# Four slots instead of two for gathered rows and their indices in a fused graph-network kernel

## The chip, the core and the metric

The kernel runs on one core of a Trainium2 chip, in float32 throughout. The core has TensorE (PE), VectorE (DVE), ScalarE (ACT), GpSimd (POOL) and SyncE (SP), which share an SBUF of 128 partitions and a PSUM of eight banks, meet through semaphores, and move data by DMA. The metric is device time in microseconds (us), as the median of several executions. Beside it there is one profiled execution, from which all rows come.

## What is computed

The graph has N = 3125 nodes with F = 64 features and E = 103125 edges, sorted by destination. Four networks follow one another, each with a residual addition and a layer norm:

```python
# 0: message network, edge weight as the edge feature
x = concatenate([h[src], h[dst], e]);  m = relu(x @ W1 + b1) @ W2 + b2
x = layernorm(x + segment_sum(m, dst))
# 1: GIN with edge features (32 per edge)
msg = relu(x[src] + edge_attr @ We + be);  aggr = segment_sum(msg, dst)
h = relu(((1 + eps) * x + aggr) @ W1 + b1) @ W2 + b2    # leaky relu, norm
x = layernorm(x + h)
# 2: three steps x <- A x with A = norm of the edge weights; 3: ten steps
msgs = norm[:, None] * x[row];  x = segment_sum(msgs, col)
agg = segment_sum(h[s] * wn[:, None], d);  h = 0.9 * agg + 0.1 * feat_0
```

Networks 0 and 1 have a function of each edge, so they are computed edge by edge. Networks 2 and 3 only multiply by a fixed sparse matrix, which the kernel builds once as a dense matrix and then multiplies by on TensorE.

## The kernel before

**Stages.** A preparation (to about 105 us) loads the graph, makes tables in DRAM of what a node contributes to an edge (`d_p`, `d_q`; later `d_t1`), and `rec`, four numbers per edge for 808 tiles of 128 edges. Then comes the edge loop of layer 0 (to about 1400 us), a short node phase, the edge loop of layer 1 (about 1438 to 2708 us), a node phase, and the dense products on TensorE (from about 2762 us), which stream a matrix `d_w` of several MB from DRAM.

**An edge loop.** It runs over 101 superblocks of 1024 edges. In numbers, superblock n uses buffer b = n % 2. `edge_loop` writes the first 96 as nested hardware loops: 6 turns of two quarters, each quarter a loop of 4 turns of two superblocks. The last 5 are written out. For each superblock the engines do this, each engine in its own program order and with semaphores between them, two of each kind, one for each b:

- SP: load 8x128 source indices (L441), once the addition of n-2 is done; in layer 0 two loads of `d_q` rows (L447), in layer 1 one of edge attributes (L451); then two copies of 16 edge records from `rec` into `wrec` (L460), once `pair_outer` of n-2 is done.
- POOL: wait for the indices (`idx`) and for TensorE's sums of n-2 (`seg`), then eight indirect DMAs of 128 rows each (L566) into `G[b]`. These are the gathers.
- DVE: `pair_low` (L669 to L671); the addition of PSUM to the gathered rows (L696), which waits for the gather; one-hot matrices of the next superblock (L654, L657); `pair_outer` (L678, L683, L685); then the aggregation (L705), which adds TensorE's sums of 47 columns to `aggT` and waits for `seg` of n.
- ACT: relu in place on the gathered rows (L1028), a copy of the transposed one-hots (L1021) or attributes (L1023), and the eviction of the dense pair (L1037, L1038).
- PE: the transposes of n+1 (L1180, L1185), 32 matmuls that sum the rows by destination (L1212, L1213, after the relu), the products of n+1 (L1195 or L1198), and 16 matmuls of a pair of 16 columns of the dense matrix (L1224).

The dense matrix is made beside the edges: 96 superblocks of layer 0 and 100 of layer 1 each make one pair. After each 8 superblocks ACT stores a finished quarter, 1 MB, to `d_w`.

**What sets the order.** Nothing is scheduled by a planner: each engine's function `superblock` is its order, and the semaphore counts are its ring. DVE first increments the semaphores `agg` and `add` by 1, so that the first two superblocks find free buffers. If the destinations are not as assumed, a fallback path (`general`) runs instead; with this input it does not.

Of the kernel before, what the change touches and what calls it, by code (L numbers as in the profile page):

```python
# [19 lines left out]
N, F, E, ED = 3125, 64, 103125, 32  # L20
P = 128
NB = -(-N // P)
NP = NB * P
SBE = 8 * P
NSB = -(-E // SBE)
# [14 lines left out]
SPAN = 47  # L40
PIECE = 4
# [18 lines left out]
NC_HT, NC_DEG, NC_LEAKY, NC_X2 = 11, 19, 24, 41  # L60
# [11 lines left out]
def build(nc, x, src, dst, eattr, ew, ew1, W1_0, b1_0, W2_0, b2_0, We, be, W1_1, b1_1, W2_1, b2_1,  # L72
# [5 lines left out]
    with ctx:  # L78
# [56 lines left out]
        o_rec = take(NT * 4)  # L135
        o_g = take(2 * 8 * F)
# [7 lines left out]
        o_idx = take(2 * 8)  # L144
# [6 lines left out]
        rec = at(o_rec, NT, 4)  # L151
        G = at(o_g, 2, 8, F)
# [11 lines left out]
        idx = at(o_idx, 2, 8).bitcast(i32)  # L164
# [30 lines left out]
        xT = at(tmp(NP), NP)  # L195

# [3 lines left out]
        genB = [at(o_alo, NCOL), at(o_g, NCOL)]  # L200
        genA = [at(o_g + NCOL + P * b, P) for b in range(2)]
        assert NCOL <= o_rec - o_alo and NCOL + 2 * P <= o_ew - o_g
# [15 lines left out]
        h1T = at(o_rec, NP)  # L218
        o_l1 = o_g
        w1n = at(o_l1, F, parts=F)  # L220
# [39 lines left out]
        d_lo = dram("d_lo", [1, NWIN], i32)  # L260
        d_w = dram("d_w", [P, NCH * CH // QC, STR, QC])
# [14 lines left out]
        s.st_q = sem("st_q")  # L276
        s.prep_v = sem("prep_v")
# [83 lines left out]
        def edge_loop(eng, layer, superblock, quarter_end=None):  # L361
            r = R[layer]
            with eng.Fori(0, NLOOP // 16) as u:
                for q in range(2):
                    with eng.Fori(0, 4) as m:
                        for b in range(2):
                            h = 8 * u + 4 * q + m
                            kh = h + layer * (NLOOP // 2)
                            superblock(r, 2 * h + b, h, b, 2 * kh + b, kh, q, 2 * m + b, u + layer * (NLOOP // 16), True)
                    if quarter_end:  # L370
                        quarter_end(2 * u + q + layer * (NLOOP // 8), q, u + layer * (NLOOP // 16))
            for i in range(NLOOP, NSB):
# [3 lines left out]
                superblock(r, i, i // 2, i % 2, k, None if k is None else k // 2, None, i - NLOOP, None, i + 1 < NSB)  # L376
# [31 lines left out]
        def start_rings(eng, names):  # L408


            for x in names:
                for each in x:
                    eng.sem_inc(each, 1)
# [3 lines left out]
        def _(sp):  # L417
# [21 lines left out]
            def superblock(r, i, h, b, k, kh, q, mb, qh, more):  # L439
                sp.wait_ge(r.add[b], h + 1)  # L440
                sp.dma_start(idx[:, b, :], rows(src, i)).then_inc(r.idx[b], 16)  # L441
# [961 lines left out]
```

## Time and profile before

| | us |
|---|---|
| median of 3 runs (lowest, highest) | 3809.07 (3807.27, 3817.12) |
| span of the profiled execution | 3796.3 |
| POOL busy in it | 1839.9 (48%) |
| PE busy in it | 2583.5 (68%) |
| DVE busy in it | 1369.5 (36%) |
| mean granted TensorE clock | 0.793 |

Only the span is recorded for the profiled execution, from its first to its last instruction; it is 12.8 us below the median of the runs. The page cuts the span into 40 slices of 95 us and gives each engine's busy share in tenths: POOL shows 6 or 7 from slice 2 to slice 28 and 0 after that, PE 5 to 7 in the same slices and 9 in the last eleven, so the two edge loops and the dense products are told apart at a glance. In the chain that ended last, POOL's L566 has 26% of the span, "issue" 18% and PE's L1353 (dense products) 23%. "Issue" is time in which an engine waited for nothing that the profile shows. "Remote" as a releaser is a semaphore event with no instruction in the record to match it.

### The profile page before, as it was taken

How to read it: one execution, taken by the hardware profiler on the slowest of the kernel's cores; microseconds unless marked ns; L12 is line 12 of the kernel's file. 1: busy time of each engine (PE TensorE's matmuls, PEld its weight loads, DVE VectorE, ACT ScalarE, POOL GpSimd, SP SyncE). 2: the span in 40 equal slices, each digit the busy share in tenths (PEclk: the TensorE clock that was granted, in tenths of full speed). 3: DMA queues.
4: the chain of work that ended last, by engine and by line, in shares of the span. 5: the costliest groups of instructions: out<-in, count | busy, mean ns of one | idle time of the engine just before them, and what ended most of it. 6: DMA issues, size and time to landing. Idle time of an engine off the chain costs nothing.

```text
span 3796.3 us, 51155 instructions
## 1 busy us (share of the span) xinstructions
PE 2583.5 (68%) x16589; PEld 1756.2 (46%) x16589; DVE 1369.5 (36%) x2536; ACT 407.4 (11%) x940; POOL 1839.9 (48%) x1633
## 2 busy tenths in 40 slices
PE   1565766665666654565656555555669799999997
PEld 1455655555555543554545454555523233333332
DVE  2433434343434324344344444444286311111112
ACT  1111111111111110111111111111100000000000
POOL 0676777676777756777777777777300000000000
PEclk7677767667777756777777777777689899999999
DMA  4211111111111121221212121211069789999997
GB/s 41 40 35 34 35 35 35 35 34 35 24 35 35 35 34 40 44 45 43 45 42 45 44 44 44 44 44 43 18 235 351 278 309 334 345 345 337 343 344 239
DMA packets 387168, 433.50 MB, mean 114 GB/s; under 512 B 184958, under 2 KB 197887, under 8 KB 384046
## 3 DMA queue, kind: packets, MB, share of 16 engines
q1 hardware_dynamic: 324860, 352.87, 28.9%
q0 software_dynamic: 51712, 53.06, 7.7%
q10 hardware_dynamic: 10546, 26.89, 1.9%
q8 instruction: 33, 0.54, 0.1%
q14 instruction: 17, 0.14, 0.0%
HBM read 401.00 MB, written 28.43 MB: 113 GB/s over the span
## 4 chain that ended last, share of the span: by engine, by line
PE 31%; POOL 26%; issue 18%; another core or an unknown queue 12%; DVE 5%; DMA 3%; DVEq 1%; SPq 1%; ACT 1%; POOLq 0%; ACTq 0%
POOL arena L566 26%; PE bank L1353 23%; PE bank L1212 2%; PE bank L1329 1%; DMA arena<-in_edge_weight 1%; PE bank L1224 1%; DMA arena<-d_p,arena 1%; PE bank L1180 1%; DVE arena L654 1%; DVEq L690 1%; DVE arena L696 1%; PE bank L1195 1%; DVE arena L670 0%; DVE arena L671 0%
## 5 line engine op out<-in xcount | busy, mean ns | idle before, releaser
L566 POOL DMA_INDIRECT arena<-d_p,arena x808 | 919.4, 1138 | 396.9 <-issue 364.9
L566 POOL DMA_INDIRECT arena<-d_t,arena x808 | 911.8, 1128 | 393.3 <-issue 352.9
L1353 PE MATMUL bank<-arena 128*64 128x512 f32 (+1 forms) x4550 | 916.1, 543 | 59.2 <-DVE arena L879 33.3
L1224 PE MATMUL bank<-arena 128*128 128x200 f32 x3136 | 758.0, 397 | 79.4 <-issue 77.8
L1224 PEld LDWEIGHTS bank<-arena 128*128 128x128 f32 x3136 | 704.1, 241 | 134.4 <-issue 117.9
L1212 PE MATMUL bank<-arena 128*64 128x47 f32 x3232 | 341.1, 295 | 539.4 <-ACT arena L1028 411.0
L1353 PEld LDWEIGHTS bank<-arena 128*64 128x64 f32 x4550 | 304.3, 136 | 615.3 <-issue 552.8
L1212 PEld LDWEIGHTS bank<-arena 128*64 128x64 f32 x3232 | 313.3, 198 | 594.9 <-issue 326.6
L685 DVE TENSOR_TENSOR arena<-arena 128x1600 f32<-128x1600 f32 x196 | 358.0, 1826 | 6.8
L1213 PE MATMUL bank<-arena 128*64 128x47 f32 x3232 | 344.3, 295 | 3.6 <-issue 3.6
L1180 PE MATMUL bank<-arena 128*96 128x128 f32 x404 | 89.8, 364 | 367.5 <-DVE arena L657 224.0
L705 DVE TENSOR_TENSOR arena<-bank,arena 128x47 f32 x202 | 41.8, 207 | 809.2 <-remote 704.7
L696 DVE TENSOR_TENSOR arena<-bank,arena 128x512 f32<-128x512 f32 x202 | 139.1, 689 | 502.0 <-DMA arena<-d_t,arena 268.1
L1213 PEld LDWEIGHTS bank<-arena 128*64 128x64 f32 x3232 | 313.2, 198 | 4.7 <-issue 4.7
L924 DVE TENSOR_TENSOR arena<-bank,arena 128x256 f32<-128x256 f32 (+1 forms) x70 | 27.7, 396 | 621.7 <-PE bank L1329 621.7
L1180 PEld LDWEIGHTS bank<-arena 128*96 128x96 f32 x404 | 54.6, 161 | 400.5 <-DVE arena L657 230.0
L670 DVE TENSOR_TENSOR arena<-arena 128x1024 f32<-128x1024 f32 x196 | 239.1, 1220 | 0.4 <-issue 0.4
L1037 ACT ACTIVATE arena<-bank 128x144 f32 x192 | 55.9, 291 | 1643.3 <-PE bank L1224 932.1
L1195 PE MATMUL bank<-arena 96*128 96x128 f32 x808 | 193.3, 397 | 37.1 <-issue 32.9
L1198 PE MATMUL bank<-arena 128*128 128x256 f32 x404 | 198.3, 643 | 0.5 <-issue 0.5
L1195 PEld LDWEIGHTS bank<-arena 96*128 96x128 f32 x808 | 159.9, 286 | 49.1 <-issue 40.6
L1028 ACT ACTIVATE arena<-arena 128x512 f32<-128x512 f32 x202 | 127.3, 630 | 474.3 <-DVE arena L696 443.3
(152 smaller groups left out, 1324.8 us busy)
## 6 DMA issues: line engine op xcount, KB each, us to landing
arena<-d_w SPq DMA_DIRECT2D x312, 1024.0 KB, 9.0
d_w<-arena ACTq DMA_DIRECT2D x24, 1024.0 KB
arena<-d_p,arena POOLq DMA_INDIRECT x808
arena<-in_edge_attr SPq DMA_DIRECT2D x101, 128.0 KB
arena<-d_t,arena POOLq DMA_INDIRECT x808
arena<-arena SPq DMA_DIRECT2D x392, 8.0 KB
arena<-in_src SPq DMA_DIRECT2D x202, 4.0 KB
arena<-d_q SPq DMA_DIRECT2D x202, 11.8 KB
```

Source lines behind the costliest of these rows:

```text
L566: g.indirect_dma_start(G[:, b, j, :], None, table, bass.IndirectOffsetOnAxis(ap=idx[:, b, j:j + 1], axis=0)).then_inc(r.g[b], 16)
L670: d.tensor_tensor(alo[:, b], bc(0, P), iota.unsqueeze(1).to_broadcast([P, 2 * TPW, P]), ALU.is_equal).then_inc(s.pair_step, 1)
L685: d.tensor_tensor(outer[:, b].rearrange("p t (c j) -> p t c j", j=WIN), hi1.unsqueeze(3).to_broadcast([P, 2 * TPW, NB, WIN]), dsel.unsquee ...
L696: d.tensor_tensor(gflat, psPre[b][:, :], gflat, ALU.add).then_inc(r.add[b], 1)
L1028: a.activation(gflat, gflat, ACT.Relu).then_inc(r.relu[b], 1)
L1180: last = t.transpose(psT[0:2 * (SPAN + 1), P * j:P * j + P], OH[:, b, 2 * j:2 * j + 2, :].rearrange("p k c -> p (k c)"), ident)
L1195: last = t.matmul(psPre[b][:, P * j:P * j + P], OHT[:, b, P * j:P * j + P], QD[:, b, :], start=True, stop=True)
L1198: last = t.matmul(psPre[b][:, 2 * P * j:2 * P * j + 2 * P], EAT[:, b, P * j:P * j + P], WEBD, start=True, stop=True)
L1212: t.matmul(psSeg[0:F, P * b:P * b + SPAN], G[:, b, j, :], OH[:, b, j, 0:SPAN], start=j == 0, stop=j == 7)
L1213: last = t.matmul(psSeg[F:P, P * b:P * b + SPAN], beside.to_broadcast([P, F]), OH[:, b, j, 0:SPAN], start=j == 0, stop=j == 7)
L1224: last = t.matmul(prod[:, :, WIN * w:WIN * w + WIN], alo[:, b, TPW * w + j, :], outer[:, b, TPW * w + j, :].rearrange("p (c j) -> p c j", ...
L1353: last = t.matmul(banks[t_ % 4][F * (n % 2):F * (n % 2) + F, 0:w_], old[:, n, :], right, start=n < 2, stop=n >= NB - 2)
```

## The change

`G` and `idx` get four slots each. The two edge loops' hardware loops have 2 turns of four superblocks in place of 4 turns of two, slot = n % 4, while everything else keeps its two buffers. POOL waits for `idx` of the slot and for DVE's `agg` of four superblocks back instead of PE's `seg` of two back; SP loads indices after the `add` of four back. So `add` and `agg` start at 2 and each other wait on them is shifted by one.

To make room, `rec` becomes a temporary of the preparation and is stored in DRAM (`d_rec`) once; SP then loads the 16 records of each window from there. The fallback path loads its own copy. `h1T` moves, and DVE clears `accL` once more in the second node phase.

```diff
+SLOTS = 4
-        o_rec = take(NT * 4)
-        o_g = take(2 * 8 * F)
+        o_g = take(SLOTS * 8 * F)
-        o_idx = take(2 * 8)
+        o_idx = take(SLOTS * 8)
-            r.idx = two(f"idx{layer}")
-            r.g = two(f"g{layer}")
+            r.idx = [sem(f"idx{layer}_{slot}") for slot in range(SLOTS)]
+            r.g = [sem(f"g{layer}_{slot}") for slot in range(SLOTS)]
-                    with eng.Fori(0, 4) as m:
-                        for b in range(2):
-                            h = 8 * u + 4 * q + m
+                    with eng.Fori(0, 2) as m:
+                        for slot in range(SLOTS):
+                            b = slot % 2
+                            g4 = 4 * u + 2 * q + m
+                            h = 2 * g4 + slot // 2
@@ sync
+            sp.wait_ge(s.rec_c, 8)
+            sp.dma_start(d_rec, rec).then_inc(s.st_rec, 16)
                 sp.wait_ge(r.add[b], h + 1)
-                sp.dma_start(idx[:, b, :], rows(src, i)).then_inc(r.idx[b], 16)
+                sp.dma_start(idx[:, slot, :], rows(src, i)).then_inc(r.idx[slot], 16)
-                    sp.wait_ge(s.rec_c, 8)
+                    sp.wait_ge(s.st_rec, 16)
                         sp.dma_start(wrec[:, b, w * TPW:(w + 1) * TPW, :],
-                                     rec[:, ds(lo, TPW), :]).then_inc(s.wrec[b], 16)
+                                     d_rec[:, ds(lo, TPW), :]).then_inc(s.wrec[b], 16)
@@ gpsimd
-                pool.wait_ge(r.idx[b], 16 * (h + 1))
-                pool.wait_ge(r.seg[b], h + 1)
+                pool.wait_ge(r.idx[slot], 16 * (g4 + 1))
+                pool.wait_ge(r.agg[b], h + 1)
                 for j in range(8):
-                    g.indirect_dma_start(G[:, b, j, :], None, table,
+                    g.indirect_dma_start(G[:, slot, j, :], None, table,
@@ vector
-            start_rings(v, [s.pair_v, [s.pair_step]] + [x for r in R for x in (r.agg, r.add, [r.m_agg])])
+            start_rings(v, [s.pair_v, [s.pair_step]] + [x for r in R for x in ([r.m_agg],)])
+            start_rings(v, [x for r in R for x in (r.agg, r.add)], SLOTS // 2)
-                v.wait_ge(r.g[b], P * (h + 1))
+                v.wait_ge(r.g[slot], P * (g4 + 1))
-                v.wait_ge(r.agg[bn], hn + 1)
+                v.wait_ge(r.agg[bn], hn + SLOTS // 2)
+            link2(d.memset(accL, 0.0))
@@ scalar
-                act.wait_ge(r.add[b], h + 1 + 1)
+                act.wait_ge(r.add[b], h + 1 + SLOTS // 2)
@@ tensor
-                pe.wait_ge(r.add[b], h + 1)
+                pe.wait_ge(r.add[b], h + SLOTS // 2)
-                pe.wait_ge(r.agg[b], h + 1)
+                pe.wait_ge(r.agg[b], h + SLOTS // 2)
```

POOL's program, one turn of the inner loop of layer 0. Before, it stands so; `seg0_1` is the semaphore of PE's sums for buffer 1 in layer 0, `idx0_1` that of the index load, and a row with x7 is the other seven gathers of a superblock:

```order
L365 ISA
L566 DMA arena<-d_p,arena 128x64 [waits idx0_0,seg0_0]
L566 DMA arena<-d_p,arena 128x64 x7
L566 DMA arena<-d_p,arena 128x64 [waits idx0_1,seg0_1]
L566 DMA arena<-d_p,arena 128x64 x7
L365 REGISTER_ALU
```

Of the change (L566 is now L578), with `agg0_0` the semaphore of DVE's aggregation for buffer 0:

```order
L575 ISA [waits idx0_0]
L578 DMA arena<-d_p,arena 128x64 [waits agg0_0]
L578 DMA arena<-d_p,arena 128x64 x7
L578 DMA arena<-d_p,arena 128x64 [waits idx0_1,agg0_1]
L578 DMA arena<-d_p,arena 128x64 x7
L575 REGISTER_ALU [waits idx0_2]
L578 DMA arena<-d_p,arena 128x64 [waits agg0_0]
L578 DMA arena<-d_p,arena 128x64 x7
L578 DMA arena<-d_p,arena 128x64 [waits idx0_3,agg0_1]
L578 DMA arena<-d_p,arena 128x64 x7
L370 REGISTER_ALU
```

A turn has four groups of eight gathers, each group waits for its own slot's indices, and the second wait is DVE's.

SP's program at the join of one superblock and the next, before:

```order
L460 ISA [waits pair_v_0]
L460 DMA arena<-arena 128x16
L457 ISA
L457 TENSOR_LOAD arena
L457 ISA x2
L460 ISA
L460 DMA arena<-arena 128x16
L441 ISA [waits add0_1]
L441 DMA arena<-in_src 128x8
```

and of the change:

```order
L470 ISA [waits pair_v_0]
L470 DMA arena<-d_rec 128x16
L467 ISA
L467 TENSOR_LOAD arena
L467 ISA x2
L470 ISA
L470 DMA arena<-d_rec 128x16
L451 ISA [waits add0_1]
L451 DMA arena<-in_src 128x8
```

The place of the index load is the same: behind the record loads of the superblock before it, which wait for `pair_v`. The records now come from DRAM, and the same wait on `add` means the addition of four superblocks back.

## Rows read from the trace of the kernel before

**Rows 1.** Part 5: costliest groups (line, engine, operation xcount | busy, mean ns | idle before).
```profile
L566 POOL DMA_INDIRECT arena<-d_p,arena x808 | 919.4, 1138 | 396.9 <-issue 364.9
L566 POOL DMA_INDIRECT arena<-d_t,arena x808 | 911.8, 1128 | 393.3 <-issue 352.9
...
L705 DVE TENSOR_TENSOR arena<-bank,arena 128x47 f32 x202 | 41.8, 207 | 809.2 <-remote 704.7
```
**Rows 2.** Busy time by stage: window, length, each engine, PEclk, DMA share, GB/s.
```profile
105.00:1400.00 1295.00, 817.30 (x5948) 714.75 (x5947) 502.92 (x975) 172.94 (x393) 919.38 (x808) 0.70 0.17 34
...
1438.00:2708.00 1270.00, 741.14 (x5438) 650.75 (x5438) 516.08 (x1001) 148.97 (x402) 911.75 (x808) 0.77 0.19 43
...
2762.00:3796.00 1034.00, 960.22 (x4875) 338.87 (x4875) 287.59 (x470) 61.48 (x105) 0.00 (x0) 0.96 0.91 318
```
**Rows 3.** One line's instructions, L566: duration ns min/median/max, first and last start.
```profile
L566 POOL DMA_INDIRECT arena<-d_p,arena x808: 942/947/2607, 105.8 to 1397.6; - x162
L566 POOL DMA_INDIRECT arena<-d_t,arena x808: 942/947/2596, 1438.7 to 2702.7; - x162
```
**Rows 4.** Timeline of POOL, 2591 to 2620 us (start, us, instruction, [idle before]).
```profile
2592.63 0.95 POOL L566 DMA_INDIRECT arena<-d_t,arena  x1 [2.22 <-issue]
...
2596.80 2.02 POOL L566 DMA_INDIRECT arena<-d_t,arena  x1 [0.30 <-issue]
...
2603.20 0.95 POOL L566 DMA_INDIRECT arena<-d_t,arena  x1 [0.30 <-issue]
...
2614.00 0.95 POOL L566 DMA_INDIRECT arena<-d_t,arena  x1 [0.31 <-issue]
2617.39 0.95 POOL L566 DMA_INDIRECT arena<-d_t,arena  x1 [2.44 <-issue]
```
**Rows 5.** Timeline of DVE, 2591 to 2620 us.
```profile
2596.18 1.83 DVE L685 TENSOR_TENSOR arena<-arena 128x1600 f32<-128x1600 f32 x1
2597.92 0.20 DVE L705 TENSOR_TENSOR arena<-bank,arena 128x47 f32 x1
...
2605.64 0.69 DVE L696 TENSOR_TENSOR arena<-bank,arena 128x512 f32<-128x512 f32 x1 [4.54 <-DMA arena<-d_t,arena]
...
2616.77 0.21 DVE L705 TENSOR_TENSOR arena<-bank,arena 128x47 f32 x1 [7.64 <-remote]
```
**Rows 6.** Timeline of PE, 2603 to 2620 us.
```profile
2608.87 0.32 PE L1213 MATMUL bank<-arena 128*64 128x47 f32 x1
2609.12 2.08 PE L1198 MATMUL bank<-arena 128*128 128x256 f32 x4
```
**Rows 7.** Timeline of POOL, 1005 to 1036 us.
```profile
1010.59 2.60 POOL L566 DMA_INDIRECT arena<-d_p,arena  x1 [2.08 <-issue]
```
**Rows 8.** Timeline of SP, 2591 to 2620 us.
```profile
2606.52 0.35 SPq L441 DMA_DIRECT2D arena<-in_src  x1
...
2610.69 1.99 SPq L460 DMA_DIRECT2D arena<-arena  x2
```
**Rows 9.** Timeline of SP, 30 to 112 us.
```profile
71.75 1.94 SPq L430 DMA_DIRECT2D arena<-in_dst  x1
73.73 10.90 SPq L431 DMA_DIRECT2D arena<-in_edge_weight  x1
...
99.20 0.69 SPq L436 DMA_DIRECT2D d_q<-arena  x1
102.16 0.39 SPq L441 DMA_DIRECT2D arena<-in_src  x1
```
**Rows 10.** All DMA issues: KB each, median us from issue to landing.
```profile
arena<-in_edge_weight SPq DMA_DIRECT2D x3, 404.0 KB, 16.8
...
d_p<-arena SPq DMA_DIRECT2D x1, 288.0 KB, 5.0
...
arena<-in_L_gnn_We SPq DMA_DIRECT2D x4, 8.0 KB, 2.0
```
**Rows 11.** Part 3: DMA queue: packets, MB, share.
```profile
q8 instruction: 33, 0.54, 0.1%
```

More of the change, by code:

```diff
@@ L195, in build @@
         xT = at(tmp(NP), NP)
+        rec = at(tmp(NT * 4), NT, 4)
         iotaW = at(o_stage, NP)
-        genB = [at(o_alo, NCOL), at(o_g, NCOL)]
-        genA = [at(o_g + NCOL + P * b, P) for b in range(2)]
-        assert NCOL <= o_rec - o_alo and NCOL + 2 * P <= o_ew - o_g
+        genB = [at(o_alo, NCOL), at(o_alo + NCOL, NCOL)]
+        genA = [at(o_alo + 2 * NCOL + P * b, P) for b in range(2)]
+        genrec = at(o_alo + 2 * NCOL + 2 * P, NT, 4)
+        assert 2 * NCOL + 2 * P + 4 * NT <= o_ew - o_alo
         gen_row = at(o_agg, NCH * CH)
@@ L260, in build @@
         d_lo = dram("d_lo", [1, NWIN], i32)
+        d_rec = dram("d_rec", [P, NT, 4])
         d_w = dram("d_w", [P, NCH * CH // QC, STR, QC])
@@ L436, in _, with superblock @@
                 sp.dma_start(d_q.rearrange("(a p) f -> p a f", p=P)[:, lo_:hi_, :], PQ[:, lo_:hi_, F:P]).then_inc(s.st_q, 16)
+            sp.wait_ge(s.rec_c, 8)
+            sp.dma_start(d_rec, rec).then_inc(s.st_rec, 16)
             sp.wait_ge(s.flag, 1)
[L439 removed]
+            def superblock(r, i, h, b, slot, g4, k, kh, q, mb, qh, more):
                 sp.wait_ge(r.add[b], h + 1)
[L441 removed]
+                sp.dma_start(idx[:, slot, :], rows(src, i)).then_inc(r.idx[slot], 16)
                 if r is R[0]:
@@ L479, in general0 @@
             def general0():
+                sp.wait_ge(s.st_rec, 16)
+                sp.dma_start(genrec, d_rec).then_inc(s.gen_rec, 16)
                 sp.wait_ge(s.gen_st, 16 * STR)
@@ L687, in pair_outer, with superblock @@
                                 dsel.unsqueeze(2).to_broadcast([P, 2 * TPW, NB, WIN]), ALU.mult).then_inc(s.pair_v[b], 1)
-            def superblock(r, i, h, b, k, kh, q, mb, qh, more):
+            def superblock(r, i, h, b, slot, g4, k, kh, q, mb, qh, more):
                 base = v.value_load(base_row[0:1, ds(i, 1)], min_val=0, max_val=N - 1)
@@ L1023, in product_copy, with superblock @@
                     a.activation(EAT[:, b, :], psT[:, 0:2 * P], ACT.Copy).then_inc(r.trc[b], 1)
-            def superblock(r, i, h, b, k, kh, q, mb, qh, more):
-                act.wait_ge(r.add[b], h + 1 + 1)
-                gflat = G[:, b].rearrange("p k f -> p (k f)")
+            def superblock(r, i, h, b, slot, g4, k, kh, q, mb, qh, more):
+                act.wait_ge(r.add[b], h + 1 + SLOTS // 2)
+                gflat = G[:, slot].rearrange("p k f -> p (k f)")
                 a.activation(gflat, gflat, ACT.Relu).then_inc(r.relu[b], 1)
@@ L1199, in products, with superblock @@
                 last.then_inc(r.pre[b], 1)
-            def superblock(r, i, h, b, k, kh, q, mb, qh, more):
+            def superblock(r, i, h, b, slot, g4, k, kh, q, mb, qh, more):
                 hn, bn = following(h, b)
```

39 lines of the change are left out of this document (21 added, 18 removed).

## Prediction, made before the changed kernel ran

> **What bounds the kernel now.** I read the busy time by stage first. The two edge loops last 1295 and 1270 us for 101 superblocks each, 12.82 and 12.57 us a superblock [rows 2]. The dense products (1034 us) have POOL at nothing and PE at 960 us; the change leaves them as they are. In the edge loops no engine is full by busy time, POOL nearest with 919 of 1295 us [rows 2]. But POOL's gathers do not follow each other without space: the groups of part 5 give 808 of them at a mean of 1138 and 1128 ns [rows 1], and the timeline shows 0.30 us ahead of each one that waits for nothing [rows 4]. So a superblock's eight gathers occupy 8 x (1.138 + 0.30) = 11.50 us in layer 0 and 8 x (1.128 + 0.30) = 11.42 in layer 1, of 12.8 and 12.6. From the start of the first gather to the end of the last are 1397.6 + 0.95 - 105.8 = 1292.8 us in layer 0 and 1265.0 in layer 1 [rows 3]; 808 x 1.438 = 1162 and 808 x 1.428 = 1154 of it are gathers and their fixed space, so 131 + 111 = 242 us are waits. That is all that more slots can give back.
>
> What POOL waits for is seen in one cycle of two superblocks. POOL starts at 2592.63, sends 16 gathers, ends at 2614.95 and starts again at 2617.39, after 2.44 us [rows 4]: 24.76 us, 12.38 each. DVE's addition starts at 2605.64, 1.5 us after the eighth gather ended at 2604.15 [rows 4, 5]: DVE waits for the rows to land, so in this half the gather is what is late. PE's sums end at 2609.19 and PE's queue goes on with the next products [rows 6], but DVE's aggregation, which waits for just these sums, starts at 2616.77, 7.64 us idle, "remote" [rows 5]. POOL waits for the same sums and starts at the same moment. One superblock earlier the aggregation started at 2597.92, directly behind its predecessor [rows 5]. Over the whole run the idle time put down to "remote" before L705 is 704.7 us [rows 1]. The signal of PE is thus seen late in every second superblock, 1.8 us after POOL's last queued gather ended (2614.95). No row says what holds it; that it comes just when POOL has run dry is the most important fact for this change.
>
> **The change part by part.**
>
> POOL's waits. With four slots, gather n needs the aggregation of n-4 and the indices of n. The aggregation of n-4 lies two superblocks further back than the sums of n-2. The late aggregation of 2616.77 would be needed only when POOL has two more superblocks behind it, 23 us after 2614.95. So if the lateness stays at 8 us, the 242 us of waits go, but for two things. First, a pause of about 2 us that comes once in a while (one at 1010.59, with a first gather of 2.60 instead of 0.95 us [rows 7]); they come every 112 gathers, 1616/112 = 14 of 2.08 us, 29 us. Second, whatever indices come late, which I put at nothing: SP issued the index load at 2606.52, directly after the addition at 2605.64, and the two record copies at 2610.69 to 2612.68 [rows 8]; behind those stands the next index load, whose `add` is long done with four slots. POOL needs it some 15 us later, a landing of 8 KB takes 2.0 us [rows 10]. What the two windows hold ahead of the first gather and behind the last, 2565 - 1292.8 - 1265.0 = 7 us, stays. The sum: 101 x (11.50 + 11.42) = 2315, plus 29, plus 7 = 2351 us, against 2565 now: minus 214 us.
>
> How much of the mean duration is real for the changed kernel: the median gather takes 0.947 us and the longest 2.6 [rows 3]. Long ones coincide with DVE's large instruction: the gather of 2.02 us at 2596.80 lies beside L685, 2596.18 to 2598.01 [rows 4, 5]. DVE's work per superblock does not change, so I keep the mean; were it gone, the loop would be 202 x 8 x 1.25 = 2020 us. The Trainium skill ("SBUF — State Buffer", section "Who interferes with whom") says that a tensor_tensor, having no two-port mode, was not seen to hold up descriptor generation, only copies and casts were; by that rule the mean would fall towards the median whenever DVE's copies are elsewhere, and the loops to 2020 us. The trace speaks against it with the 2.02 us beside L685, a tensor_tensor, and I do not count on it.
>
> The other engines. PE is busy 7.7 us a superblock ((817.3 + 741.1)/202) at a granted clock of 0.70 to 0.77 [rows 2], part at each of its two levels, 1.2 and 2.4 GHz. An estimate for all of it at 1.2 GHz: 7.7 x 0.735/0.5 = 11.3 us, just under 11.5. DVE is busy 5.0 us. ACT 1.6. So POOL stays the bound, with little to spare: a chain of addition, relu, sums, products that can't overlap with the pair matmuls would give about 12 us (a rival below).
>
> The records. Two copies a superblock become loads from DRAM of the same 8 KB. The trace has no such load of 128 pieces of 64 bytes; the nearest is 2.0 us for 8 KB [rows 10], the far one 5.0 us for 288 KB [rows 10]. They are issued at 2612.68 at the latest and used by `pair_low` of the superblock after next, over 8 us later, so I count 0, with up to 202 x 0.3 us = 60 us if DRAM is slow enough to make DVE late in a part of them. The store of `d_rec`, 404 KB, stands on SP behind the issue at 99.20 and before the index load at 102.16 [rows 9]. An issue of that size took between 1.94 and 10.90 us [rows 9], and one of 1.94 would just fit between 99.9 and 102.2. I take +1 us, up to +9; landing (16.8 us at most [rows 10]) delays the first `pair_low`, once. DVE's memset on the node chain: +0.2 us, like another small DVE instruction [rows 1]. Half the loop branches go: while POOL is the bound, the other engines' branches are hidden beside its gathers, and I count 0 for POOL's own, of which there are 96 in 1616 gathers.
>
> Sum: 3796.3 - 214 + 1 = 3583 us for the profiled span; the median is 12.8 us above it now, so 3596. **I say 3600 us.**
>
> **The rivals.**
>
> Held signals (slower). Whatever holds PE's signal may last as long as POOL keeps sending, since it ended 1.8 us after the last gather of the 16 and was absent where the sums came within 6 us of POOL's restart [rows 4 to 6]. With two slots POOL runs dry after 16 gathers by itself; with four it has up to 32 in front of it, 46 us. After a restart two or three superblocks pass, then the next sums are held until POOL has used all free slots. If three pass, a cycle would be 3 x 11.5 + 2.5 = 37 us, 12.3 each, hardly another time than now. But now the indices are late: the load for the next free slot stands behind SP's record copies of the superblock before it, which wait for `pair_outer` of a superblock that DVE reaches only after the held aggregation. From addition to the end of these copies are 7 us (2605.64 to 2612.68 [rows 5, 8]), and 2 us to land, so POOL pauses 11 us instead of 2.4: (46 + 11)/4 = 14.3 us a superblock, 202 x 14.3 + 7 = 2896 us, plus 331, about 4140 us; halfway to now, at 13.5, about 3980. It decides from the point at which a signal given more than some 14 us after POOL's restart is still seen late while POOL sends. For it speaks the coincidence with POOL running dry, against it that POOL no longer waits for PE's semaphore at all, and that its cause is not in the rows.
>
> A smaller gain. PE at the low level or the chain decides at about 12.1 us a superblock: 202 x 12.1 + 7 = 2451, minus 114, about 3695 us. For it: PE's 11.3 us above. Against: the addition at 2605.64 had waited 4.54 us for its gather [rows 5], so that the chain was ahead of POOL.
>
> No change. Held signals cost with three superblocks a cycle what they cost now, and pauses of 4 to 5 us: 12.7 us a superblock, 3809 us within its error.
>
> Code loading. Each engine's loop body doubles and the turns fall from 48 to 24 a layer. The profile shows 33 instruction packets in the whole span [rows 11], so the loops are not loaded anew at each turn now; if they were after, at 2 us (the 8 KB load [rows 10]) for 48 turns, it would be at most 96 us back of the gain, 3692 us. The Trainium skill ("Runtime: NRT & Kernel Launch", section "Instruction fetch mechanics") says that a taken branch to a target outside the resident window must wait for a fetch. By that rule a longer body is the one that suffers; 3% is what I give it.
>
> **How the numbers follow.** About 0.3% (11 us) is what a measurement of this kernel can tell from no change. POOL-bound, 3565 to 3650 us: 0.43, the likeliest, so the time is 3600. Smaller gain (0.08) and code loading (0.03), 3650 to 3797: 0.11. No change: 0.13. Held signals with a loss, 3825 to 4180: 0.32, evenly spread. What is left, 0.01, goes to slower: faster 0.54, same 0.13, slower 0.33. The range of 8 in 10 has to reach into the slower case: 3575 leaves 0.05 below, 4100 about 0.10 above. For the likeliest case alone it is 3565 to 3650.
>
> **What would show it.** Right: POOL's busy share in the edge loops 8 tenths instead of 6 to 7, idle before the changed L566 near 550 us, windows of 1180 us per edge loop, aggregations held 8 us but with POOL not pausing behind them. Wrong by held signals: "remote" idle before DVE's aggregation above 1500 us, single waits of 15 to 30 us, POOL's pauses of 8 us and more after runs of 24 to 32 gathers. Smaller gain: DVE's addition no longer waits for the gather but for PE's products, at a granted clock of 0.5 to 0.6. The dense products should stand at 1034 us and the first gather at 106 to 116 us; if not, my costs of the store or the records are wrong.

## The result

| | before | changed |
|---|---|---|
| median, us (lowest, highest) | 3808.36 (3807.27, 3817.12), 4 runs | 4110.28 (4092.93, 4122.81), 4 runs |
| ratio, 95% interval | | 1.079 [1.076, 1.082], slower |
| span of the profiled execution, us | 3796.3 | 4121.0 |
| edge loop, first to last gather, us: layer 0, layer 1 | 1292.8, 1265.0 | 1410.0, 1447.7 |
| mean granted TensorE clock | 0.793 | 0.765 |

The forecast was 3600 us, and 4110 lies just outside of the range that I gave, 3575 to 4100. What came is nearest to the first rival, priced at 4140.

The changed kernel's profile, stage by stage (window, length, busy time of each engine, PEclk, DMA share, GB/s); these answer to [rows 2]:

```profile
108.80:1519.00 1410.20, 738.33 (x5900) 664.07 (x5900) 499.28 (x971) 160.31 (x391) 877.89 (x808) 0.70 0.15 31
1519.00:1565.40 46.40, 17.88 (x126) 16.74 (x126) 18.43 (x24) 4.89 (x6) 0.00 (x1) 0.50 0.33 32
1565.40:3013.00 1447.60, 707.06 (x5344) 604.04 (x5345) 507.98 (x989) 138.94 (x395) 864.18 (x808) 0.70 0.17 38
...
3080.00:4121.00 1041.00, 962.04 (x4875) 338.75 (x4875) 291.40 (x474) 61.36 (x105) 0.00 (x0) 0.96 0.91 315
```

Of the 324.7 us between the two spans, 300 are in the edge loops: 1410.0 + 1447.7 against 1292.8 + 1265.0 [rows 3]. Most of the rest lies between and behind the loops: from the last gather of layer 0 to the first of layer 1 are 46.6 us for 40.1, from the last gather to the first dense product (the first start of L1368 and, before, L1353) 96.0 for 83.5. From that product to the end it is 1011.9 us for 1009.2, so the products are as they were. The busy times of POOL, PE and DVE in the loops did not rise, so it is all waiting.

Part 5 of the changed kernel, the lines that answer to [rows 1]; L578 and L718 are the gathers and the aggregation:

```profile
L578 POOL DMA_INDIRECT arena<-d_t,arena x808 | 864.3, 1070 | 630.0 <-DMA arena<-in_src 387.7
L578 POOL DMA_INDIRECT arena<-d_p,arena x808 | 877.9, 1086 | 559.2 <-DMA arena<-in_src 310.4
...
L718 DVE TENSOR_TENSOR arena<-bank,arena 128x47 f32 x202 | 41.8, 207 | 1502.4 <-remote 1206.4
```

The gathers got shorter, 1078 ns for 1133. But POOL's idle time is 1189 us for 790, and 698 of them end with an index load (`in_src`), where it was 64 in the kernel before. DVE's idle time before the aggregation put down to "remote" has grown from 704.7 to 1206.4 us. The waits of DVE and of POOL (waited for: us in total, times, longest) say how:

```profile
DVE arena L718 <- remote: 1206.4, 103, 31.9
```
```profile
POOL arena L578 <- DMA arena<-in_src: 698.1, 70, 46.6
```

There are not more late signals (103 for 96), each lasts longer: 11.7 us on average, 31.9 at most, where it was 7.3 and 8.7. I had put "above 1500 us" under the signs of held signals; that total was too high, while single waits and pauses (40 of more than 8 us inside the loops) came as written there.

**One cycle.** POOL's timeline, where it stops for 10.56 us and then sends 24 gathers, up to the one at 1014.87:

```profile
982.23 0.94 POOL L578 DMA_INDIRECT arena<-d_p,arena  x1 [10.56 <-DMA arena<-in_src]
985.02 1.13 POOL L578 DMA_INDIRECT arena<-d_p,arena  x1 [1.86 <-issue]
...
991.45 0.94 POOL L578 DMA_INDIRECT arena<-d_p,arena  x1 [0.30 <-issue]
992.69 0.95 POOL L578 DMA_INDIRECT arena<-d_p,arena  x1 [0.30 <-issue]
...
1014.87 0.95 POOL L578 DMA_INDIRECT arena<-d_p,arena  x1 [0.30 <-issue]
1028.80 1.11 POOL L578 DMA_INDIRECT arena<-d_p,arena  x1 [12.98 <-DMA arena<-in_src]
```

DVE's timeline in it (L709 is the addition, L698 the large instruction of `pair_outer`):

```profile
992.35 0.21 DVE L718 TENSOR_TENSOR arena<-bank,arena 128x47 f32 x1 [7.01 <-remote]
996.54 0.69 DVE L709 TENSOR_TENSOR arena<-bank,arena 128x512 f32<-128x512 f32 x1 [1.54 <-remote]
...
1018.46 0.21 DVE L718 TENSOR_TENSOR arena<-bank,arena 128x47 f32 x1 [18.44 <-remote]
1021.03 0.68 DVE L709 TENSOR_TENSOR arena<-bank,arena 128x512 f32<-128x512 f32 x1
...
1022.67 1.83 DVE L698 TENSOR_TENSOR arena<-arena 128x1600 f32<-128x1600 f32 x1
```

PE's timeline: the sums of that superblock begin at 1002.31, the products behind them at 1004.19; L1239 are the matmuls of the dense pair:

```profile
1002.31 0.34 PE L1227 MATMUL bank<-arena 128*64 128x47 f32 x1 [3.40 <-issue]
1004.19 2.34 PE L1210 MATMUL bank<-arena 96*128 96x128 f32 x8
1006.87 4.35 PE L1239 MATMUL bank<-arena 128*128 128x200 f32 x12 [0.34 <-issue]
1011.88 0.76 PE L1239 MATMUL bank<-arena 128*128 128x200 f32 x3 [0.66 <-issue]
1013.99 0.33 PE L1239 MATMUL bank<-arena 128*128 128x200 f32 x1 [1.34 <-issue]
```

And SP's:

```profile
1003.94 0.00 SPq L451 DMA_DIRECT2D arena<-in_src  x1
1018.54 0.64 SPq L457 DMA_DIRECT2D arena<-d_q  x2
1024.68 1.56 SPq L470 DMA_DIRECT2D arena<-d_rec  x2
1026.43 0.33 SPq L451 DMA_DIRECT2D arena<-in_src  x1
```

Read together: POOL's last gather ends at 1015.82. PE went from the sums to the next products by 1004.2, but DVE sees the sums only at 1018.46, 14 us later and 2.6 us after POOL ran dry. Near the end PE's own instructions start ever further apart, with 0.34, 0.66 and 1.34 us of "issue" ahead of them. SP stood behind `pre`, PE's signal too, until 1018.54, then for `pair_outer`, which DVE ended at 1024.5, and only behind its record loads came the index load, at 1026.43. POOL starts 2.4 us later. So the pause is 12.98 us where the same event cost 2.44 [rows 4]: nobody gathers while the held work is made up for, because the indices of the next gather hang on it.

Not every late signal waits for POOL to stop. The one ahead of this, seen by DVE at 992.35 after 7.01 us, came between two gathers 0.30 us apart. Over the whole run 70 of the 103 late waits ended so, while gathers went on: 7.5 us on average, 17.2 at most, 528 us together. The other 33 ended while POOL stood still: 20.6 us on average, up to 31.9, 679 us together. In the kernel before it was 8 and 88. POOL waits there for the same sums as DVE, so that it must stop when they are late enough.

### The profile page after: what moved, and what is told of

Its sections match the earlier page's. It is cut to its first block, busy times and chain, and to the rows that moved or that the text cites. A ratio compares the mean times of both kernels' runs of the same rounds, so it can differ in the third digit from the quotient of the medians.

```text
span 4121.0 us, 50949 instructions
## 1 busy us (share of the span) xinstructions
PE 2487.5 (60%) x16589; PEld 1672.2 (41%) x16589; DVE 1365.3 (33%) x2537; ACT 387.7 (9%) x940; POOL 1750.9 (42%) x1633
## 4 chain that ended last, share of the span: by engine, by line
another core or an unknown queue 36%; PE 34%; issue 11%; DVE 7%; ACT 3%; DMA 3%; DVEq 2%; POOL 2%; SPq 2%; ACTq 0%; POOLq 0%
PE bank L1368 22%; PE bank L1239 4%; PE bank L1227 3%; POOL arena L578 2%; DVE arena L698 1%; ACT arena L1042 1%; PE bank L1210 1%; PE bank L1344 1%; DMA arena<-in_edge_weight 1%; DVEq L703 1%; DVE arena L709 1%; PE bank L1213 1%; DVE arena L667 1%; DVE arena L684 1%
## 5 line engine op out<-in xcount | busy, mean ns | idle before, releaser
L578 POOL DMA_INDIRECT arena<-d_t,arena x808 | 864.3, 1070 | 630.0 <-DMA arena<-in_src 387.7
L578 POOL DMA_INDIRECT arena<-d_p,arena x808 | 877.9, 1086 | 559.2 <-DMA arena<-in_src 310.4
L1368 PE MATMUL bank<-arena 128*64 128x512 f32 (+1 forms) x4550 | 917.9, 544 | 60.4 <-DVE arena L893 33.5
L1227 PE MATMUL bank<-arena 128*64 128x47 f32 x3232 | 321.4, 284 | 881.9 <-ACT arena L1042 578.4
L1239 PE MATMUL bank<-arena 128*128 128x200 f32 x3136 | 731.4, 386 | 106.4 <-issue 105.0
L1239 PEld LDWEIGHTS bank<-arena 128*128 128x128 f32 x3136 | 669.2, 230 | 159.1 <-issue 147.2
L1227 PEld LDWEIGHTS bank<-arena 128*64 128x64 f32 x3232 | 292.9, 187 | 944.3 <-issue 575.6
L1368 PEld LDWEIGHTS bank<-arena 128*64 128x64 f32 x4550 | 304.1, 136 | 618.4 <-issue 554.0
L718 DVE TENSOR_TENSOR arena<-bank,arena 128x47 f32 x202 | 41.8, 207 | 1502.4 <-remote 1206.4
L698 DVE TENSOR_TENSOR arena<-arena 128x1600 f32<-128x1600 f32 x196 | 358.1, 1827 | 6.8
L1228 PE MATMUL bank<-arena 128*64 128x47 f32 x3232 | 323.5, 284 | 8.7 <-issue 8.6
L1228 PEld LDWEIGHTS bank<-arena 128*64 128x64 f32 x3232 | 293.4, 187 | 5.6 <-issue 5.6
L1210 PE MATMUL bank<-arena 96*128 96x128 f32 x808 | 177.2, 378 | 40.7 <-issue 35.5
L709 DVE TENSOR_TENSOR arena<-bank,arena 128x512 f32<-128x512 f32 x202 | 138.7, 687 | 153.4 <-remote 106.2
L1213 PE MATMUL bank<-arena 128*128 128x256 f32 x404 | 173.2, 563 | 17.4 <-issue 17.2
L1210 PEld LDWEIGHTS bank<-arena 96*128 96x128 f32 x808 | 149.2, 272 | 54.3 <-issue 42.0
```

Of the source, the lines that this page charges most:

```text
L578: g.indirect_dma_start(G[:, slot, j, :], None, table, bass.IndirectOffsetOnAxis(ap=idx[:, slot, j:j + 1], axis=0)).then_inc(r.g[slot], 16)
L698: d.tensor_tensor(outer[:, b].rearrange("p t (c j) -> p t c j", j=WIN), hi1.unsqueeze(3).to_broadcast([P, 2 * TPW, NB, WIN]), dsel.unsquee ...
L709: d.tensor_tensor(gflat, psPre[b][:, :], gflat, ALU.add).then_inc(r.add[b], 1)
L1210: last = t.matmul(psPre[b][:, P * j:P * j + P], OHT[:, b, P * j:P * j + P], QD[:, b, :], start=True, stop=True)
L1213: last = t.matmul(psPre[b][:, 2 * P * j:2 * P * j + 2 * P], EAT[:, b, P * j:P * j + P], WEBD, start=True, stop=True)
L1227: t.matmul(psSeg[0:F, P * b:P * b + SPAN], G[:, slot, j, :], OH[:, b, j, 0:SPAN], start=j == 0, stop=j == 7)
```

## The experiments

Five sets of runs, each beside the kernel before on its own chip. In four of them, and beside the changed kernel, the kernel before took 3802 to 3810 us. In the first set it took 3542 to 3554 us in its 16 runs, with a median of 3545, and none of the four kernels traced in that set shows a "remote" wait before the aggregation (the kernel before has no trace from it). The first two sets ran on a chip of the same number (3), the third and fourth on number 0, the fifth on number 6; what differed between the first two isn't known to me. So a table by set; comparisons are made inside one. "Remote" is the idle time before DVE's aggregation so labelled, and its longest.

| set | kernel | median us | before | ratio [95%] | remote, longest |
|---|---|---|---|---|---|
| 1 | depth 2 | 3535 | 3545 | 0.997 [0.996, 0.999] | none |
| 1 | early indices | 3539 | 3545 | 0.998 [0.997, 0.999] | none |
| 1 | memset 2600 | 4048 | 3545 | 1.141 [1.139, 1.143] | none |
| 1 | no gathers | 2550 | 3545 | 0.719 [0.717, 0.721] | none |
| 2 | before again | 3802 | 3802 | 0.999 [0.997, 1.002] | 742, 9.5 |
| 2 | changed again | 4118 | 3802 | 1.081 [1.077, 1.084] | 1255, 30.4 |
| 2 | depth 2 | 3765 | 3802 | 0.989 [0.986, 0.993] | 744, 9.6 |
| 2 | early indices | 3837 | 3802 | 1.006 [1.003, 1.010] | 888, 30.6 |
| 3 | memset 2600 | 4061 | 3810 | 1.066 [1.061, 1.071] | 33, 8.6 |
| 3 | no gathers | 2546 | 3810 | 0.669 [0.666, 0.672] | none |
| 3 | depth 3, early indices | 3829 | 3810 | 1.004 [1.001, 1.006] | 904, 19.4 |
| 3 | depth 2, early indices | 3772 | 3810 | 0.991 [0.988, 0.994] | 736, 10.4 |
| 4 | memset 900 | 3800 | 3806 | 0.999 [0.996, 1.001] | 385, 9.8 |
| 4 | memset 128 | 3805 | 3806 | 1.000 [0.998, 1.001] | 446, 21.9 |
| 4 | memset 900 each 16 | 3811 | 3806 | 1.001 [0.999, 1.003] | 878, 22.5 |
| 5 | two slots, records | 3785 | 3808 | 0.994 [0.992, 0.997] | 704, 9.0 |
| 5 | and bodies of four | 3762 | 3808 | 0.989 [0.986, 0.993] | 739, 9.3 |
| 5 | depth 2 | 3774 | 3808 | 0.991 [0.989, 0.993] | 748, 9.6 |

**Is it the depth?** The depth is the number of superblocks that POOL may be ahead. Here POOL waits for PE's sums of two superblocks back as well:

```diff
                 pool.wait_ge(r.agg[b], h + 1)
+                pool.wait_ge(r.seg[b], h + 1)
```

> The changed kernel with one wait added: POOL also waits for PE's sums of two superblocks back (seg), as the kernel before did, so that it may not run further ahead than before, though it has four slots. Loops of four superblocks, records in DRAM and the index loads stay as changed. Theory A (the loss comes from POOL's longer runs of gathers, during which PE's signals are seen late): the time is the kernel before's, 3800 to 3825 us, 'remote' idle before DVE's aggregation near 705 us, longest 9 us. Theory B (the loss comes from the doubled loop bodies, the records from DRAM or the store): the time stays at 4050 to 4130 us.

> The changed kernel with POOL also waiting for PE's sums of two superblocks back, once more. Where signals are held (kernel before at about 3809 us): 3800 to 3825 us if the depth is what loses the time, 4050 and more if it is the other parts of the change. Where they are not (3545 us): 3535 us as in the first set.

In set 1, 3535 us said nothing on this, since no signal was late ("held") there. In set 2 it took 3765 us, with the changed kernel at 4118 in the same set. One wait takes 353 us away. Everything else of the change is still in. Theory B is out, and so far as the loss goes theory A is right; that the time fell below the kernel before, it did not say (the fifth set is on that).

**Is it the late indices?** SP's loads stand two superblocks earlier in its order:

```diff
-                sp.wait_ge(r.add[b], h + 1)
-                sp.dma_start(idx[:, slot, :], rows(src, i)).then_inc(r.idx[slot], 16)
+                    ahead = (slot + 2) % SLOTS
+                    sp.wait_ge(r.add[b], h + 2)
+                    sp.dma_start(idx[:, ahead, :], rows(src, i + 2)).then_inc(r.idx[ahead], 16)
@@ the last two superblocks load nothing; 0 and 1 are loaded ahead of the loop
```

> The changed kernel, with SP's index loads issued two superblocks earlier in SP's order (the first two ahead of the loop, then those of superblock n+2 where those of n stood). POOL's waits on 'in_src' are 698 us of idle time in the changed kernel. Theory A1 (late indices, pushed back behind the record loads, are what turns a held signal into a loss): these waits fall below 50 us, POOL's pauses to 2.5 us, a superblock to some 12.3 us, 3720 to 3800 us. Theory A2 (the held signals alone set the time, the indices only come as late as everything else): POOL waits the same time for agg instead, 4050 to 4130 us. In between, 3850 to 4000 us, where both have a part. The longest 'remote' wait before DVE's aggregation stays near 30 us in either.

> The changed kernel with SP's index loads two superblocks earlier in its order, once more. Where signals are held: 3720 to 3800 us if the late indices turn the held signals into a loss, 4050 to 4130 us if the held signals alone set the time. Where they are not: 3538 us as in the first set.

3837 us in set 2, 281 less than the changed kernel, with the waits of its aggregation (L728) and of its gathers (L588):

```profile
DVE arena L728 <- remote: 887.8, 108, 30.6
```
```profile
POOL arena L588 <- DVE arena L728: 123.3, 32, 9.0
POOL arena L588 <- DMA arena<-in_src: 78.7, 2, 51.5
```

The longest hold is as long as ever, 30.6 us, but POOL no longer stands behind the indices: the 78.7 us left are before the first gathers. So A1 holds for 281 of the 353 us, while its number was too good: I had 3720 to 3800. Of the rest, 123.3 us are waits for the held aggregation, and "issue" rose from 491 to 658 us. The other 72 us are what the depth costs with early indices: 0.6% over the kernel before, where a depth of two is 1.1% under it. A depth of three costs about as much as four, 0.4% over in its set:

> The changed kernel with index loads two superblocks earlier and POOL waiting for DVE's aggregation of three superblocks back instead of four, so a run of gathers is at most some 24 long. Where signals are held: if each hold lasts until POOL has sent all it may, the longest 'remote' wait is some 20 us (9 at a depth of two, 31.9 at four) and the time is between 3765 (depth two) and 3837 us (depth four, early indices), 3770 to 3830 us. If the depth makes no difference once the indices are early, 3837 us or more. Where they are not held: 3538 us.

The longest hold there is 19.4 us, as expected, between 10.4 (two, with early indices) and 30.6 (four). The longest hold grows with the longest run of gathers that POOL may send. The sum of the holds does not: 736, 904 and 888 us.

**Does it belong to the program?**

> The kernel before, unchanged, for its trace on the chip of this set of runs. In the set ahead of this one the kernel before took 3545 us, where it had taken 3809 beside the changed kernel, and none of the kernels run with it showed a single 'remote' wait before DVE's aggregation. Theory D (the held signals belong to one chip or its state at the time, not to the program): where this kernel takes about 3545 us its trace has no 'remote' waits before L705 and POOL's gathers follow each other without pauses, 11.4 to 11.5 us a superblock; where it takes about 3809 us it has some 700 us of them.

> The changed kernel, unchanged. Theory D: where the kernel before takes about 3545 us, the changed one takes 3530 to 3550 us (POOL is then the bound in both, with nothing for more slots to give); where the kernel before takes about 3809 us, it takes 4090 to 4125 us. Rival (the loss comes from the program itself, say its late index loads or longer bodies, and shows on any chip): 7 to 8% above the kernel before in either case, that is about 3825 us beside 3545.

The kernel before and the changed one, repeated in set 2, came out within 0.2% of their first times, at 3802 and 4118 us. So about 8% is what the change costs where signals are held. Theory D's other half has one set to stand on: the changed kernel as it is was not run there, only its two relatives at 3535 and 3539 us, 0.2 to 0.3% under the kernel before, though one has the full depth of four. Without held signals the slots give nothing, because POOL was hardly stopped at a depth of two: 8.5 us of waits for PE and DVE in the whole run. The gathers of the kernel with early indices (first and last start) show the bare bound:

```profile
L588 POOL DMA_INDIRECT arena<-d_p,arena x808: 940/944/2019, 109.2 to 1262.2; - x162
L588 POOL DMA_INDIRECT arena<-d_t,arena x808: 940/944/2487, 1303.9 to 2437.1; - x162
```

That is 1154 and 1134 us, 11.3 a superblock, 2.4% under my 2315 + 29 us. None of its gathers has more than 0.3 us of "issue" ahead of it, so the 29 us of rare pauses did not come there at all, and the mean gather took 1112 ns.

**Do POOL's gathers hold the signals?** POOL issues none, and SP loads 1024 fixed rows in one DMA instead:

```diff
@@ sync, behind the index load
+                sp.wait_ge(r.agg[b], h + 1)
+                sp.wait_ge(s.st_p if r is R[0] else s.st_t1, 32 if r is R[0] else 16)
+                sp.dma_start(G[:, slot], (d_p if r is R[0] else d_t1)[0:SBE, :]
+                             .rearrange("(p k) f -> p k f", k=8)).then_inc(r.g[slot], 16)
@@ gpsimd
-                pool.wait_ge(r.agg[b], h + 1)
-                for j in range(8):
-                    g.indirect_dma_start(G[:, slot, j, :], None, table, ...
@@ vector
-                v.wait_ge(r.g[slot], P * (g4 + 1))
+                v.wait_ge(r.g[slot], 16 * (g4 + 1))
```

> The changed kernel without gathers: POOL issues none, and SP loads 1024 fixed rows of the same table with one direct DMA into each slot (the gather itself is left out, the bytes are the same). All other work stays. Theory A (POOL's gathers hold PE's signals): 'remote' waits before DVE's aggregation nearly vanish (below 50 us of 1206) and the edge loops run at the pace of PE and DVE, 8 to 11 us a superblock, 3000 to 3500 us in all. Theory C (the signals are late for a reason that has nothing to do with POOL, such as PE's own queue): remote waits of 8 us and more stay in at least a quarter of the superblocks.

> The changed kernel without POOL's gathers, once more: one direct DMA on SP's queue brings 1024 fixed rows of the same table per superblock (the gather is left out). Where signals are held for the other kernels: if POOL's gathers hold them, this one has no 'remote' waits and takes 2550 us as in the first set; if PE's or the chip's own state does, it has them too and takes 2700 us or more.

2550 us in set 1 and 2546 in set 3, where the others were held, with no "remote" wait before the aggregation in either. So the gathers are needed for PE's signals to be late. They are not enough, since in set 1 they held nothing, and the edit takes away two things at once, POOL's instructions and the DMA queue that they fill; which of them it is was not tested. It also prices the rest of an edge loop: (2546 - 3796 + 2558)/202 = 6.5 us a superblock by the spans of before outside the loops, at a mean clock of 0.95 (0.98 in the loops). At that clock PE and DVE are far from being the bound. And in set 1, at 0.75 and 0.80 in the two loops, they never stopped the early-index kernel's gathers. My 11.3 us for a low clock was thus not reached as a limit in any run.

**What lets a signal through?** A POOL memset of its own behind each eight gathers:

```diff
+                pool.wait_ge(s.pause, i + 1 + (0 if r is R[0] else NSB))
+                pool.nop(nofuse=True)
                 for j in range(8):
                     g.indirect_dma_start(...)
+                g.memset(scratch, 0.0).then_inc(s.pause, 1)   # not behind the very last; pause starts at 1
```

> The changed kernel with one POOL memset of 128x2600 (about 2.2 us of POOL's own work) behind each eight gathers, so that POOL sends nothing for some 2.7 us after each superblock but does not wait. Theory A (a signal of PE is held only while gathers are sent one after another for long, and a pause in the sending lets it through): no 'remote' wait before DVE's aggregation above 10 us, and a period of 11.3 + 2.7 = 14.0 us of POOL, 202 x 14.0 = 2830 us of edge loops, about 4050 to 4110 us, with the remote sum below 400 us of 1206. Theory A' (what lets the signal through is that POOL's program stands at a wait, or that all gathers have landed): the memset does not help, remote waits of 20 to 35 us stay, and the time goes up by 2.2 x 202 = 440 us or nearly, 4400 to 4550 us.

> The changed kernel with the POOL memset of 128x2600 (2.28 us in the first set) behind each eight gathers, once more: in the first set no signal was held, even in the kernel before (3545 us), so it told nothing of the holding. Where signals are held (kernel before near 3800 us): if a pause in the sending of gathers lets them through, POOL's work is 202 x (11.3 + 2.3 + 0.7) and the time that of the first set, 4040 to 4080 us, with no 'remote' wait above 10 us; if POOL has to stand at a wait for that, remote waits of 20 us and more stay, and the time is 4300 to 4550 us.

4061 us in set 3, as in set 1 (4048), where nothing was held. POOL's timeline in set 3:

```profile
1010.54 2.28 POOL L586 MEMSET arena<- 128x2600 f32 x1
1013.58 0.97 POOL L583 DMA_INDIRECT arena<-d_p,arena  x1 [0.76 <-POOL arena L586]
...
1024.74 2.29 POOL L586 MEMSET arena<- 128x2600 f32 x1
1027.78 0.95 POOL L583 DMA_INDIRECT arena<-d_p,arena  x1 [0.75 <-POOL arena L586]
```

and the aggregation's late signals over the whole run:

```profile
DVE arena L725 <- remote: 33.1, 6, 8.6
```

33 us against 1206 in the changed kernel. POOL is idle for no more than 0.76 us at a time here, so it does not have to run dry at a wait; 3.0 us without a gather in 14.2 are enough. How much less will do was asked with early indices:

> Four slots, index loads two superblocks earlier, and a POOL memset of 128x900 (some 0.85 us) behind each eight gathers. If any break of a microsecond in the sending lets signals through: no 'remote' waits above 5 us, POOL the bound at 11.35 + 0.85 + some 0.45 for the wait = 12.3 to 12.6 us a superblock, 3730 to 3800 us. If the break has to be longer than the 1.5 us that a gather takes to land: remote waits of 10 to 30 us stay as without the memset, 3840 to 3950 us.

> The same with a memset of 128x128 (some 0.2 us). Short break enough: 11.35 + 0.2 + 0.45 = 12.0 us a superblock, 3660 to 3700 us, faster than every version so far. Not enough: remote waits stay as in the version with early indices alone, 3810 to 3850 us.

> The memset of 128x900 behind each sixteen gathers only. If a break of 0.9 us lets the signals through: holds end at it, no 'remote' wait above 10 us, and with four slots POOL does not run dry, 11.35 + 0.65 = 12.0 us, 3660 to 3700 us. If not: 3830 to 3900 us with waits of 20 us and more.

The aggregation's waits, one kernel each in this order:

```profile
DVE arena L734 <- remote: 385.2, 110, 9.8
```
```profile
DVE arena L734 <- remote: 446.2, 51, 21.9
```
```profile
DVE arena L734 <- remote: 877.9, 107, 22.5
```

None of the expectations held as a whole: it is neither a threshold at 1.5 us nor does any break do. (The first, 3800 us, stands at the edge of its range, but with waits up to 9.8 us; the third has the waits of 20 us and more, but not the time.) With breaks of 3.0, 1.6 (0.87 + 0.75) and 1.0 us (0.22 + 0.75) behind eight gathers, and of 1.6 behind sixteen, "remote" is 33, 385, 446 and 878 us, against 888 with none: it grows as gathers get denser. A held signal thus does not need an event, POOL's stop, to come through, as the 70 waits that ended between gathers show too; more likely something falls behind while gathers come one every 1.43 us, and catches up in the gaps. And all of it comes out at the same time, 3800, 3805 and 3811 us: what the breaks save in holds they cost in gathers. What it is that falls behind, the records don't show, and I leave it open; so also why it did not in the first set.

**What is left of the change at a depth of two?**

```diff
-SLOTS = 4
+SLOTS = 2          # records stay in DRAM, POOL waits for seg of two back
-                    with eng.Fori(0, 2) as m:     # second kernel: unchanged
+                    with eng.Fori(0, 4) as m:     # first kernel: bodies of two
```

> The changed kernel taken back to two slots, loops of two superblocks and POOL waiting for PE's sums of two back: against the kernel before, only the records from DRAM (with the store, and the memset) are left. If the 8 KB copies inside SBUF disturbed the edge loops: 3765 to 3785 us beside 3800 to 3810. If the records are neutral, as I priced them: 3795 to 3812 us.

> The same with loop bodies of four superblocks, two slots. If half the branches bring something (1 us at most for each of 48 turns saved on PE or DVE in the loops): 10 to 40 us under the run with records alone. If they are hidden, as I priced them: the same time within 10 us. If longer bodies cost instruction loading: slower than the run with records alone.

> The changed kernel with POOL kept to two superblocks ahead, in one set with the two above: 3760 to 3772 us where signals are held. What it has below the run with two slots and bodies of four is what the four slots bring without the depth: if nothing, the two are the same within 10 us.

The records from DRAM (with their store) give 23 us (0.6%, [0.3, 0.8]), bodies of four another 23, between intervals that just touch, and the four slots at a depth of two nothing: 3774 us against 3762, with intervals that overlap. Both edits that I had priced at 0 are small gains. Which wait they shorten I did not trace.

**The best version.**

> The candidate: the changed kernel with POOL kept to two superblocks ahead (it also waits for PE's sums of two back) and index loads two superblocks earlier. Where signals are held: 3750 to 3770 us, 1.0 to 1.4% under the kernel before; the indices are never late at that depth, so the second edit should bring nothing over 3765 us. Where they are not held: 3530 to 3540 us, 0.1 to 0.4% under it.

3772 us: early indices add nothing where POOL can't run ahead. The fastest of all are two slots with records in DRAM and bodies of four, 3762 us, 1.1% under the kernel before, and four slots kept to a depth of two, 3765 and 3774 us in two sets, 1.1 and 0.9% under it; the latter was also 0.3% under it where nothing was held.

## Why the prediction was wrong

**The bound.** Right where no signal is late: POOL's gathers are then the bound, with about the 242 us of waits to give back. In the first set the kernel before itself ran at 3545 us, 264 less (that its waits were gone is concluded from its time and from the kernels traced beside it), and the loops of the changed kernel's relative took 2288 us where my sum had 2344.

**The step that failed** is "so if the lateness stays at 8 us, the 242 us of waits go". It did not stay: 11.7 us on average and up to 31.9. I had the fact in hand, the hold ending as POOL ran dry, and called it the most important one, and yet took its length for a property of the signal. For 70 of the 103 late signals that was about right, 7.5 us on average. The other 33, which ended with POOL stopped, grew with its run of gathers, from 7.6 to 20.6 us. In a trace in which POOL mostly runs dry after 16 gathers, a hold of 8 us can't be told from one that lasts as long as POOL sends; I gave the first 0.43 and the second 0.32, and of the 96 late waits of that trace only 8, which ended while POOL sent, speak for the first. The kernel with early indices, which has this lateness without the late loads, took 3837 us, 237 above the forecast.

**Indices, put at nothing.** Wrong, and the larger part of the loss, 281 us, from 3837 to 4118. It is a part only together with the lateness: at a depth of two early indices gained nothing. I let SP's order pass because `add` is long done with four slots. But the load stands behind two record loads that wait for `pair_outer`, and SP is held at `pre` before them. The rival had it: a pause of 11 us a cycle, measured 10.56, 12.98, 10.27 and 4.66 in neighbouring cycles. That its sum of 4140 us came so near to 4110 is in part luck, for its parts are further off: it had each cycle at 32 gathers, and runs of 16, 24 and 32 mix, POOL's own time fell to 11.0 us a superblock from 11.5 (gathers of 1078 ns, as DVE's large instructions fall into the pauses more often, see below), and a superblock came to 14.1 us, (1410.0 + 1447.7)/202, where I had 14.3.

**Gathers lengthened beside DVE.** With the same number of DVE instructions, the mean gather went from 1133 to 1078 ns as POOL spent more time idle, and stayed at 1112 in the early-index kernel of set 1. The mean depends on what DVE's two large instructions (128x1600 and 128x1024) meet. Before, 700 of the 1616 gathers overlapped one and took 1.38 us on average, the others 0.95; in the changed kernel 495 did, at 1.38 and 0.94. That goes with the row of 2.02 us. The Trainium skill ("SBUF — State Buffer", section "Who interferes with whom") says that a tensor_tensor was not seen to stall a DMA of POOL, though with both inputs in SBUF, as here, it contends with GpSimd's reads; the trace does not agree with the first.

**Records and store.** The store is not 404 KB but four times that, 3232 words on 128 partitions, my error; its issue took 1.32 us and it landed in 8.4, and the first gather started at 108.8 for 105.8, so +3.0 where I had +1, inside my bound. The loads cost nothing, as forecast, and the two edits together gave 45 us that I had not.

**Code loading.** 37 instruction packets for 33 [rows 11], and in a second such queue, which I had left out, 23 for 17, with bodies twice as long: not fetched at each turn. The rival is out; the kernel with bodies of four and two slots is even the faster one. By the rule of the Trainium skill ("Runtime: NRT & Kernel Launch", section "Instruction fetch mechanics") the longer bodies would then still lie in the resident window.

**The other rivals.** A smaller gain through PE's chain: out, since the rest of a superblock takes 6.5 us, and in set 1 the gathers never waited for it. No change: 3829 to 3837 us is what the depth would have given with early indices, so this rival, with its 12.7 us a superblock (12.8 measured there), describes that kernel rather well.

## What to carry to other kernels

A wait that nearly always ends when some engine runs dry (88 of 96 here) may hang on that engine, even if no row says so; deeper buffers let that engine run on and can lengthen it, so price it at the full new depth too, and look at the few waits that ended otherwise. When a queue gets more slots, follow what fills them (here the index loads) back through its issuing engine's order: in-order SP had put them behind loads that hang on the very work being late. And take away the wait that seems to bind by the cheapest edit that leaves the rest in place: one added wait told more than any change of size.

## What the runs showed of the hardware

- PE's signals to DVE, ACT and SP came late, DVE waiting up to 31.9 us for one, while POOL sent indirect DMAs one every 1.4 us or so. It waited so for 33 us in all when eight gathers were followed by 3.0 us without one, and not once in the two traces of the kernel without gathers.
- In the changed kernel 70 of 103 late signals came through between gathers 0.30 us apart, after 7.5 us on average, and 33 after POOL had stopped, after 20.6 us.
- The kernel before took 3545 us in one set (16 runs) and 3802 in the next, on a chip of the same number; the traced kernels of the first show no late signal before DVE's aggregation, those of the second do.
- A gather that overlapped a float32 tensor_tensor of 128x1600 or 128x1024 took 1.38 us on average, another 0.95.
- In a long run of gathers the starts of PE's matmuls drew apart too, up to 1.34 us of "issue" between two in the cycle shown.
